# The low parts of the expert weights: one GpSimd subtraction of 1088 columns as two of 544

## The chip, the cores and the metric

The kernel runs on one core of a Trainium2 chip. The metric is the device time of one execution in microseconds (us), median of several runs. The engines are TensorE (PE), VectorE (DVE), ScalarE (ACT), GpSimd (POOL) and SyncE (SP), each with its own instruction stream; they meet only in semaphores.

## The reference

Input x has 2 x 1024 tokens of 256 features. The result is the sum of x, a log-space gated recurrence on the normalised x, and a mixture of 8 experts with the top 2 of each token:

```
xn = layernorm(x)
out = x + attn(xn) + ffn(xn)
# attn: k = xn @ W_z.T + b_z; cumsum over features, cumlogsumexp over time,
#       one mean and deviation over everything, exp, + xn, layernorm * ln_w + ln_b
# ffn, for each expert e of 8 (hidden 704):
h = silu(x @ w1[e].T) * (x @ w3[e].T)
out = out + h @ w2[e].T * expert_weight
```

## The kernel before

The first 63 us normalise x, compute the router's choice and the projections of the attention part. Then follow the expert tiles: the tokens are sorted by expert into tiles of 128, each tile belonging to one expert, 36 tiles (j = 0 to 35) in this input. All engines run the same loop over j, and the attention part is spread over the tiles by hand (functions `between`, `after`, `exp_log_first` and so on, with fixed tile numbers).

One tile goes like this. TensorE multiplies the gathered rows with w1 and w3 (`up`, 18 products at L1301), transposes the next tile's rows (L1270), multiplies the previous tile's hidden values with w2 (`down`, 18 products at L1319), and transposes the gated values (`h_tile`, 6 at L1331). ScalarE takes the silu (L608), copies the high part of x (L575), scales the result of `down` (L634), copies the high part of the transposed h (L603). VectorE multiplies the gate (L976), forms the low part of x (L967) and of h (L971), and in between does the attention's long elementwise steps on 128x1024 (L936, L941, L994, L1006, L1013), its scans (L983, L1000) and the last normalisation (L1069, L1074). TensorE's transposes (L1331) wait for the gate L976, that waits for L608.

Every product is made of fp32r values in two parts, high and low, so each weight is held as a high part and a low part. An expert's weights, WALL = 4352 columns, come by DMA into `raw` (SyncE, L339, and a small tail, L341) and are split in PIECES = 4 pieces of WP = 1088 columns: ScalarE rounds a piece to its high part (L617), GpSimd forms the low part as raw minus high (L425). Both do so behind a tile, in `split_due`: a table `plan` made on the chip says how many pieces are to be done before which tile (two at the start of an expert, one behind each of the next two tiles, for the next expert). Expert 0 is split by VectorE at the start; 7 experts x 4 pieces = 28 are done in the loop. GpSimd signals each piece (`s_w`); TensorE waits for it before it uses the expert, and SyncE before it loads the next expert's raw weights over that piece. ScalarE starts on an expert when all five loads of it have landed (`s_raw`).

GpSimd's stream in a tile is: gather of the rows of tile j + 4 (L390, an indirect DMA), scatter of tile j - 1 into the result with addition (L406), then the pieces due. Scatters wait for the landing of the one before. In tiles 28, 30 and 32 the attention part is added to the result by plain DMAs with addition (L414, `add_attention`), which also wait for scatters and are waited for by them, and there the pieces come before the scatter (`split_first`). The last tile's scatter is L470.

Of the kernel before, what the change touches and what calls it, by code (L numbers as in the profile page):

```python
# [32 lines left out]
WALL = WMAIN + D  # L33
LOADS = 5 * 16
PARTS_OF_H = 4
PIECES = 4
WP = WALL // PIECES
# [15 lines left out]
def build_program(nc, x, small, w_main, w_tail, out, xn_dram):  # L53
    fp32, f32r, i32 = mybir.dt.float32, mybir.dt.float32r, mybir.dt.int32
    u32, bf16 = mybir.dt.uint32, mybir.dt.bfloat16
    ALU, ACT, AX = mybir.AluOpType, mybir.ActivationFunctionType, mybir.AxisListType
    ds = bass.ds
    ctx = ExitStack()
    with ctx:
        def sb(name, shape, dt=fp32):  # L60
            return ctx.enter_context(nc.sbuf_tensor(name, shape, dt))

        def sem(name):
            return ctx.enter_context(nc.semaphore(name))
# [12 lines left out]
        wflat = wbuf[:, :, :, :].rearrange("p s h n -> p (s h n)")  # L77
        raw = sb("raw", [P, WALL])
# [61 lines left out]
        at = [0]  # L140
# [106 lines left out]
        s_w = sem("expert_pieces_ready")  # L247
# [42 lines left out]
        def hold(eng, s, value):  # L290

            eng.wait_ge(s, value)
            eng.nop(nofuse=True)
# [14 lines left out]
            if end:  # L308
                end(used)

        def wslot(e, part, a):

            return wflat[:, ds(e % 2 * (2 * WALL) + (a + part * WALL), WP)]


        @block.sync
# [28 lines left out]
        def _(pool):  # L345
            n = [0]
# [70 lines left out]
            def split_due(before, j):  # L417

                done = pool.value_load(plan[0:1, ds(j + 1, 1)], min_val=0, max_val=PIECES * (E - 1))
                with pool.If(before < done):  # L420
                    with pool.Fori(before, done) as p:
                        part = pool.snap(p % PIECES * WP)
                        hold(pool, s_hi, p + (PIECES + 1))
                        lo, hi = (wslot(p // PIECES + 1, n, part) for n in (1, 0))
                        pool.tensor_tensor(lo, raw[:, ds(part, WP)], hi.bitcast(fp32), ALU.subtract).then_inc(s_w, 1)  # L425
                return done

            for j in range(DEEP + 1):
# [1 line left out]
            pool.wait_ge(s_idx, 1)  # L430
            pool.wait_ge(s_ctl, 1)
            split_due(0, 0)

            def tile(i, u, done=None, parts=PARTS_OF_H, split_first=False):

                j = LOOP * i + (1 + u)
                if j + DEEP < NTILES:
                    gather(j + DEEP)
                if done is None:
                    done = pool.value_load(plan[0:1, ds(j, 1)], min_val=0, max_val=PIECES * (E - 1))  # L440
                if split_first:
                    done = split_due(done, j)
                scatter(j - 1, parts)
                return done if split_first else split_due(done, j)
# [32 lines left out]
        def _(act):  # L477
# [132 lines left out]
            def split_due(before, j):  # L610

                done = act.value_load(plan[0:1, ds(j + 1, 1)], min_val=0, max_val=PIECES * (E - 1))
                with act.If(before < done):
                    with act.Fori(before, done) as p:
                        part = act.snap(p % PIECES * WP)
                        hold(act, s_raw, p // PIECES * LOADS + 2 * LOADS)
                        act.activation(wslot(p // PIECES + 1, 0, part), raw[:, ds(part, WP)], ACT.Copy).then_inc(s_hi, 1)  # L617
                return done
# [817 lines left out]
```

## Time and profile before

| | |
|---|---|
| median of 3 runs | 352.63 us (350.98 to 352.78) |
| profiled execution | 352.66 us, span of the instructions 350.8 us |
| TensorE busy | 323.4 us (92%) |
| VectorE busy | 243.4 us (69%) |
| ScalarE busy | 229.2 us (65%) |
| GpSimd busy | 204.4 us (58%) |
| GpSimd's 28 subtractions (L425) | 78.7 us, mean 2822 ns |

Busy time of an engine includes time in which an instruction had begun and stood still, as for a port. Matmul ends are modelled. A time in a timeline is the start from the beginning of the span.

### The profile page before, as it was taken

What the parts mean: (1) busy time and instruction counts of PE and PEld (TensorE: products, weight loads), DVE (VectorE), ACT (ScalarE), POOL (GpSimd) and SP (SyncE); (2) the same over time, 40 slices, a digit from 0 to 9 for tenths busy, and PEclk for the clock granted to TensorE, in tenths of its full rate; (3) what the DMA queues carried; (4) which work ended last, traced back from release to release, by engine and by line L of the source; (5) the groups of instructions that cost most, each with busy time, mean ns of one, the idle gap of its engine ahead of it and who ended that gap; (6) DMA issues with size and microseconds to landing.
All of it is one profiled execution on the core that took longest, in us unless ns stands there. A gap on an engine that the chain in (4) does not pass through costs nothing.

```text
span 350.8 us, 6683 instructions
## 1 busy us (share of the span) xinstructions
PE 323.4 (92%) x1964; PEld 272.7 (78%) x1964; DVE 243.4 (69%) x430; ACT 229.2 (65%) x365; POOL 204.4 (58%) x137
## 2 busy tenths in 40 slices
PE   8998999898999999899989899999999999999950
PEld 8773474587878889788878788789998997999940
DVE  5488778989996779959889942455498767553410
ACT  2548898564889993899974349963955565443420
POOL 4600004249977763897789927765398458863531
PEclk9999969999999999999999999999999999999995
DMA  7952922005434642345346432544265265456431
GB/s 258 347 215 94 308 87 60 17 0 160 101 98 92 167 97 48 76 101 141 58 87 164 98 56 41 142 105 101 33 157 139 61 77 92 50 90 84 56 49 15
DMA packets 19087, 37.01 MB, mean 105 GB/s; under 512 B 2272, under 2 KB 13536, under 8 KB 19008
## 3 DMA queue, kind: packets, MB, share of 16 engines
q0 software_dynamic: 9168, 11.97, 21.7%
q1 hardware_dynamic: 8496, 22.56, 20.7%
q10 hardware_dynamic: 1376, 1.85, 1.5%
q8 instruction: 29, 0.48, 0.6%
q14 instruction: 18, 0.15, 0.1%
HBM read 27.45 MB, written 11.03 MB: 110 GB/s over the span
## 4 chain that ended last, share of the span: by engine, by line
PE 28%; issue 17%; ACT 15%; DVE 15%; DMA 13%; POOL 6%; POOLq 2%; ACTq 2%; DVEq 0%
PE PS L1301 9%; DMA out<-work,sidx 7%; PE PS L1195 7%; DMA out<-xrow 5%; PE PS L1319 4%; ACT L718 3%; POOL work L390 2%; PE PS L1331 2%; POOL out L406 2%; DVE tmp L976 2%; ACT tmp L608 2%; ACT L710 2%; ACT wbuf L617 2%; DVE hT L971 2%; DVE A L1013 1%
## 5 line engine op out<-in xcount | busy, mean ns | idle before, releaser
L1301 PE MATMUL PS<-wbuf,xT 128*128 128x512 f32 (+1 forms) x648 | 148.0, 382 | 4.4 <-issue 3.5
L1301 PEld LDWEIGHTS PS<-wbuf,xT 128*128 128x128 f32 x648 | 117.2, 188 | 28.3 <-issue 8.7
L425 POOL TENSOR_TENSOR wbuf<-raw,wbuf x28 | 78.7, 2822 | 27.4 <-ACT wbuf L617 26.6
L406 POOL DMA_INDIRECT out<-work,sidx x35 | 62.2, 1778 | 46.9 <-ACT work L634 24.8
L1319 PE MATMUL PS<-wbuf,hT 128*128 128x256 f32 x648 | 86.8, 288 | 0.0
L1319 PEld LDWEIGHTS PS<-wbuf,hT 128*128 128x128 f32 x648 | 79.3, 189 | 1.9 <-issue 1.9
L390 POOL DMA_INDIRECT work<-xn_dram,gidx x39 | 51.2, 1312 | 50.2 <-DVE gidx L907 36.8
L971 DVE TENSOR_TENSOR hT<-PS,hT 128x768 fp32r<-128x768 f32 x36 | 34.2, 950 | 46.1 <-ACT hT L603 45.1
L608 ACT ACTIVATE tmp<-PS 128x512 f32<-128x512 f32 x72 | 31.6, 459 | 38.8 <-PE PS L1301 38.7
L976 DVE TENSOR_TENSOR tmp<-tmp,PS 128x512 f32<-128x512 f32 x72 | 34.9, 515 | 28.8 <-ACT tmp L608 27.9
L1331 PE MATMUL PS<-ident,tmp 128*128 128x128 f32 x216 | 30.2, 276 | 6.1 <-DVE tmp L976 6.0
L634 ACT ACTIVATE work<-PS,wrow 128x256 f32<-128x256 f32 x35 | 16.4, 469 | 29.3 <-PE PS L1319 29.3
L603 ACT ACTIVATE hT<-PS 128x768 fp32r<-128x768 f32 x35 | 28.3, 810 | 10.5 <-PE PS L1331 10.5
L617 ACT ACTIVATE wbuf<-raw x28 | 30.4, 1110 | 4.7 <-issue 4.6
L1195 PE MATMUL PS<-xnT_M,small_sb 128*128 128x512 f32 x64 | 31.0, 624 | 1.7 <-ACT tmp L528 1.0
L1331 PEld LDWEIGHTS PS<-ident,tmp 128*128 128x128 f32 x216 | 23.9, 141 | 8.7 <-DVE tmp L976 7.7
L1195 PEld LDWEIGHTS PS<-xnT_M,small_sb 128*128 128x128 f32 x64 | 12.1, 202 | 14.0 <-issue 12.8
L710 ACT ACT_TABLE_LOAD x14 | 18.0, 1283 | 0.3
L718 ACT ACT_TABLE_LOAD x14 | 18.0, 1283 | 0.2
L967 DVE TENSOR_TENSOR xT<-PS,xT 128x256 fp32r<-128x256 f32 x37 | 15.5, 418 | 0.1
L575 ACT ACTIVATE xT<-PS 128x256 fp32r<-128x256 f32 x37 | 14.0, 382 | 1.6 <-PE PS L1270 1.6
L581 ACT ACTIVATE wrow<-work,first_pick 128x1 f32<-128x1 f32 x37 | 14.1, 385 | 0.0
(186 smaller groups left out, 367.3 us busy)
## 6 DMA issues: line engine op xcount, KB each, us to landing
raw<-w_main SPq DMA_DIRECT2D x24, 544.0 KB, 4.0
raw<-w_main SPq DMA_DIRECT2D x8, 416.0 KB, 3.5
xn_dram<-xrow SPq DMA_DIRECT2D x4, 516.0 KB, 5.9
out<-xrow POOLq DMA_DIRECT2D x4, 512.0 KB, 6.5
xrow<-x ACTq DMA_DIRECT2D x4, 256.0 KB, 5.8
xrow<-x SPq DMA_DIRECT2D x4, 256.0 KB, 5.2
small_sb<-small ACTq DMA_DIRECT2D x1, 768.0 KB, 8.3
work<-xn_dram,gidx POOLq DMA_INDIRECT x39, 4.1
```

What stands on the lines that cost most here:

```text
L390: pool.indirect_dma_start(xg[:, k, :], None, xn_dram, bass.IndirectOffsetOnAxis(gidx[:, j:j + 1], 0)).then_inc(s_gt[k], 16)
L406: pool.indirect_dma_start(out, bass.IndirectOffsetOnAxis(sidx[:, j:j + 1], 0), ysb[:, j % DEEP, :], None, compute_op=ALU.add).then_inc(s_s ...
L425: pool.tensor_tensor(lo, raw[:, ds(part, WP)], hi.bitcast(fp32), ALU.subtract).then_inc(s_w, 1)
L608: act.activation(sls[n], w1_ps[n], ACT.Silu).then_inc(s_silu, 1)
L617: act.activation(wslot(p // PIECES + 1, 0, part), raw[:, ds(part, WP)], ACT.Copy).then_inc(s_hi, 1)
L718: act.preload_act_table_set("silu_and_others")
L971: dve.tensor_tensor(hT[:, 1, :], hT_ps, hT[:, 0, :].bitcast(fp32), ALU.subtract).then_inc(s_hlo, 1)
L976: dve.tensor_tensor(g_hs[n], sls[n], w3_ps[n], ALU.mult).then_inc(s_g, 1)
L1195: ins = pe.matmul(PS[:, base + qo * CH:base + (qo + 1) * CH], wzh_sb[:, q, mat, qo * P:(qo + 1) * P], xnT[:, q, c * CH:(c + 1) * CH], star ...
L1301: ins = pe.matmul(PS[:, at:at + cols], xT[:, slot, xpart, q * P:(q + 1) * P], wbuf[:, w, wpart, q * 2 * F + at:q * 2 * F + at + cols], sta ...
L1319: ins = pe.matmul(y_ps, hT[:, hpart, c * P:(c + 1) * P], wbuf[:, w, wpart, W13 + c * D:W13 + (c + 1) * D], start=(c == 0 and hpart == 0 an ...
L1331: ins = pe.transpose(hT_ps[:, c * P:(c + 1) * P], g_h[:, a:a + P], ident[:, :])
```

## The change

Each piece is subtracted by two instructions of 544 columns, first half and second half, in place of one of 1088. The wait for ScalarE stands ahead of the first, the signal `s_w` behind the second. `wslot` gets a length.

```
-        def wslot(e, part, a):
+        def wslot(e, part, a, n=WP):
 
-            return wflat[:, ds(e % 2 * (2 * WALL) + (a + part * WALL), WP)]
+            return wflat[:, ds(e % 2 * (2 * WALL) + (a + part * WALL), n)]
...
                         part = pool.snap(p % PIECES * WP)
                         hold(pool, s_hi, p + (PIECES + 1))
-                        lo, hi = (wslot(p // PIECES + 1, n, part) for n in (1, 0))
-                        pool.tensor_tensor(lo, raw[:, ds(part, WP)], hi.bitcast(fp32), ALU.subtract).then_inc(s_w, 1)
+                        for at in (0, WP // 2):
+                            lo, hi = (wslot(p // PIECES + 1, n, part + at, WP // 2) for n in (1, 0))
+                            ins = pool.tensor_tensor(lo, raw[:, ds(part + at, WP // 2)], hi.bitcast(fp32), ALU.subtract)
+                        ins.then_inc(s_w, 1)
```

The instructions on GpSimd in the body of that loop, before (`hi_pieces_ready` is the semaphore `s_hi` that ScalarE signals; ISA rows are register instructions on the queue):

```order
L421 ISA
L425 ISA [waits hi_pieces_ready]
L425 ISA x2
L425 TENSOR_TENSOR wbuf<-raw,wbuf 128x1088
L421 REGISTER_ALU
L421 COMPARE_AND_BRANCH
```

and of the changed kernel, at the same place:

```order
L421 ISA
L426 ISA [waits hi_pieces_ready]
L426 ISA x2
L426 TENSOR_TENSOR wbuf<-raw,wbuf 128x544
L426 ISA x2
L426 TENSOR_TENSOR wbuf<-raw,wbuf 128x544
L421 REGISTER_ALU
L421 COMPARE_AND_BRANCH
```

Two register instructions and one subtraction have come in; nothing waits between the two. No instruction of another engine has moved; lines below L425 are two higher.

## Rows read from the trace of the kernel before

**Rows 1.** The page, busy time of TensorE: us, share, instructions.

```profile
PE 323.4 (92%) x1964; PEld 272.7 (78%) x1964; DVE 243.4 (69%) x430; ACT 229.2 (65%) x365; POOL 204.4 (58%) x137
```

**Rows 2.** Timeline of TensorE: start us, us, instruction, [idle before <-releaser].

```profile
84.54 0.88 PE L1331 MATMUL PS<-ident,tmp 128*128 128x128 f32 x6 [0.58 <-DVE tmp L976]
...
147.52 0.88 PE L1331 MATMUL PS<-ident,tmp 128*128 128x128 f32 x6 [1.15 <-DVE tmp L976]
148.79 4.12 PE L1301 MATMUL PS<-wbuf,xT 128*128 128x512 f32 x18 [0.40 <-issue]
...
193.88 0.88 PE L1331 MATMUL PS<-ident,tmp 128*128 128x128 f32 x6 [0.94 <-DVE tmp L976]
...
270.21 0.88 PE L1331 MATMUL PS<-ident,tmp 128*128 128x128 f32 x6
271.22 4.11 PE L1301 MATMUL PS<-wbuf,xT 128*128 128x512 f32 x18
...
313.50 0.82 PE L1331 MATMUL PS<-ident,tmp 128*128 128x128 f32 x6
314.07 4.10 PE L1301 MATMUL PS<-wbuf,xT 128*128 128x512 f32 x18
```

**Rows 3.** Timeline of VectorE, instructions with two operands in SBUF.

```profile
85.00 4.05 DVE L941 TENSOR_TENSOR U<-U,tmp 128x1024 f32<-128x1024 f32 x1
...
136.67 1.22 DVE L994 TENSOR_TENSOR U<-U,xnT_M 128x1024 f32<-128x1024 f32 x1
...
143.31 3.56 DVE L994 TENSOR_TENSOR U<-U,xnT_M 128x1024 f32<-128x1024 f32 x1
...
185.94 3.98 DVE L1006 TENSOR_TENSOR U<-U,xnT_M 128x1024 f32<-128x1024 f32 x1
...
266.18 3.38 DVE L1074 SCALAR_TENSOR_TENSOR xrow<-xrow,rstd,small_sb 128x256 f32<-128x256 f32 x2
...
281.43 0.88 DVE L1074 SCALAR_TENSOR_TENSOR xrow<-xrow,rstd,small_sb 128x256 f32<-128x256 f32 x2
```

**Rows 4.** Timeline of GpSimd, two pieces of tile 10.

```profile
143.16 2.63 POOL L425 TENSOR_TENSOR wbuf<-raw,wbuf  x1 [0.42 <-issue]
...
145.74 3.48 POOL L425 TENSOR_TENSOR wbuf<-raw,wbuf  x1
```

**Rows 5.** Line L425: ns min/median/max, first and last start.

```profile
L425 POOL TENSOR_TENSOR wbuf<-raw,wbuf x28: 2504/2600/3522, 74.7 to 306.0; - x28
```

**Rows 6.** The chain that ended last (two rows), then GpSimd's timeline.

```profile
284.63 9.10 DMA out<-xrow
...
293.76 0.28 POOL wbuf L425
...
288.82 5.22 POOL L425 TENSOR_TENSOR wbuf<-raw,wbuf  x2 [0.92 <-ACT wbuf L617]
...
303.30 1.37 POOL L414 DMA_DIRECT2D out<-xrow  x1 [0.49 <-issue]
...
342.63 1.57 POOL L470 DMA_INDIRECT out<-hst,scol  x1 [3.02 <-DMA out<-work,sidx]
```

**Rows 7.** GpSimd's groups by form: busy us, mean ns of one.

```profile
L464 POOL COPY scol<-sidx 128x1 uint32 x1 | 0.4, 379 | 0.0
...
L1427 POOL MEMSET const-float32-1.0<- 128x1 f32 x1 | 0.1, 101 | 0.0
```

**Rows 8.** ScalarE's timeline; then a window: us, ScalarE busy, clock, DMA.

```profile
148.43 0.81 ACT L603 ACTIVATE hT<-PS 128x768 fp32r<-128x768 f32 x1 [0.77 <-PE PS L1331]
...
148.40:178.40 30.00, 29.76 (x42) 1.00 0.42 99
```

**Rows 9.** SyncE's tail load, its time to landing (DMA issues), ScalarE's next rounding.

```profile
95.79 0.49 SPq L341 DMA_DIRECT2D raw<-w_tail  x1
...
raw<-w_tail SPq DMA_DIRECT2D x8, 64.0 KB, 3.8
...
105.09 2.11 ACT L617 ACTIVATE wbuf<-raw  x2
```

## The prediction

> **What bounds the kernel now.** I read the busy shares first, then the waits of each engine, then the timelines of TensorE, VectorE, GpSimd and ScalarE side by side for each of the 28 pieces (L425), and last the chain of work that ended last. TensorE is busy 92% of the span [rows 1], and in the expert tiles an undisturbed tile runs without a gap: its transposes (L1331) at 313.50 are followed by the next tile's first product (L1301) 0.57 us later [rows 2]. Time is lost where the transposes wait for VectorE's gate (L976): 0.58 us before 84.54, 1.15 before 147.52, 0.94 before 193.88. Such a wait costs twice, since the next L1301 then comes not 0.57 but 1.27 us (147.52 to 148.79) or 1.01 us (270.21 to 271.22) after the transposes [rows 2].
>
> Why is the gate late? An undisturbed 128x1024 subtraction on VectorE (L994) takes 1.22 us. The same line takes 3.56 us at 143.31; a like one takes 4.05 us at 85.00 and 3.98 us at 185.94, and a pair of L1074 takes 3.38 us at 266.18 against 0.88 us at 281.43 [rows 3]. All read two operands from SBUF, and each overlaps a piece on GpSimd. At 143.31 the piece had begun at 143.16 and ended at 145.79 [rows 4]; VectorE's ended at 146.87, 1.08 us behind it, about its own length. So VectorE stood still for the whole of the piece. The other direction shows too: the next piece is recorded from 145.74, 3.48 us long instead of 2.50 to 2.60 [rows 4, 5]: it was held until VectorE's ended, and then needed 149.22 - 146.87 = 2.35 us. Whoever has begun runs to its end.
>
> The end of the kernel is set by another chain. The scatters (L406) and the additions of the attention part (L414) all go through GpSimd one behind the other, each waiting for the landing of the last. From about 284 us on, the chain that ended last is theirs, and the last scatter (L470) waited 3.02 us for a DMA [rows 6]. TensorE's last stretch has room beside it.
>
> **The change, step by step.**
> 1. *GpSimd's own time.* 28 instructions of 1088 columns (2.50 us undisturbed, [rows 5]) become 56 of 544. The columns are the same; what is added is one start-up, f, per piece. The trace has no 544-column form. From below, a one-column memset takes 0.10 us in all; from above, a one-column copy takes 0.38 us [rows 7], which also holds a wait for the scatter beside it. I take f = 0.2, between the two and nearer the memset. That makes a half 1.35 us and adds 28 x 0.2 = 5.6 us to GpSimd. The Trainium skill (GPSIMD Engine Reference, section 3.1) gives 4497 ns for a two-input operation of 2048 columns; with the 2504 ns of 1088 columns here an estimate of f is 0.25 us, which would put the sum 0.1 to 0.2 us higher. The two register instructions ahead of the second half run on the queue under the first half (1.35 us), so I cost them at nothing; uncovered they would be some 0.3 us a piece.
> 2. *The pieces with nothing of VectorE's on them* (13 of 28, as I count them on the two timelines: those from 107 to 125, at 153, from 214 to 261 and the last at 306) cost nothing: TensorE is not waiting for the weights there, and the raw weights are reloaded early.
> 3. *The stall of VectorE.* If VectorE gets in between the halves, it waits at most 1.35 us for the first half and the second half waits for it. Piece by piece:
>  - **At 143.** The first half ends at 144.5, L994 ends at 145.7 instead of 146.87, the gate comes 1.15 us earlier. TensorE's wait of 1.15 goes and about 0.3 of the lengthened 1.27 [rows 2]. But ScalarE is the next late: its L603 began at 148.43 after a wait of 0.77 [rows 8], so it was free 0.77 earlier, and from 148.4 to 178.4 it was busy 29.76 of 30.00 us, up to the next place where TensorE waits. So only about 0.85 us comes through (0.77 and the slack of an issue). What the pieces at 153 and 161 free in the same stretch counts nothing, for the same reason.
>  - **At 75 to 97.** The wait of 0.58 before 84.54 and 0.6 of the longer gap behind it go: 1.2 us. The stall of 2.8 us at 85.00 [rows 3] shrinks too, and could give 0.7 more. Against it: here GpSimd's pieces are pushed behind VectorE's, the fourth by 3 to 4 us by my reckoning (four halves, each behind an operation of 1.2 us or a scan). Its last load (tail, L341) was issued at 95.79 and lands 3.8 us later at 99.6; ScalarE needs it at 105.09 [rows 9]. Of 5.5 us of room 1.5 is eaten by ScalarE being earlier and up to 4 by the piece. I take 1.3 of 1.9.
>  - **At 178 to 200.** VectorE's sequence is L1006, L971, L1013, statistics, gate, nearly without a gap. At 185.94 it stood 2.76 us; with the piece before it shifted by one half, L1006 runs before the next one starts and L1013 pays up to 1.35. The gate at 193 comes over 1.2 us earlier: wait of 0.94 and about 0.45 of the longer gap, 1.4 us [rows 2, 3]. The gates of the tile before and the tile behind are late for the same cause; I count 0.3 us for each, a choice below half of this site. Together 2.0.
>  - **At 266.** The second L1074 stood 2.50 us and stands half as long. L1331 at 270.21 had no wait on record but the longer gap: 1.01 - 0.57 = 0.44, and 0.2 of being late itself: 0.65.
>  Sum before 284 us: 0.85 + 1.3 + 2.0 + 0.65 = 4.8 us.
> 4. *The end chain.* At 288.82 two pieces (5.22 us) stand on GpSimd ahead of a scatter. The addition before that scatter landed at 293.73 and the second piece ended at 294.04: the piece was last, by 0.3 [rows 6]. It gets two start-ups, 0.4, and an L1074 of 0.44 us comes between its halves where 0.3 of waiting was: +0.15. The next piece ended at 302.81, 0.49 us ahead of L414 at 303.30, which stood behind it [rows 6]: +0.2. The third has room. So +0.75 us, with f = 0.10 +0.45, with f = 0.38 +1.3. That TensorE also gains at 292 is worth nothing, since this chain ends last.
>
> Sum: the profiled execution took 352.66 us (span 350.8); 352.66 - 4.8 + 0.75 = 348.6 us. Its time is that of the median of the three runs, 352.63, so I forecast 348.6, 1.1% faster. The case's own range is 346.9 to 350.6: 4.8 may be 2.8 (the sites at 85 and 193 at 0.3 and 1.0) or 6.2 (at 1.9 and 2.8), with 0.75 and 0.45 for the end chain.
>
> **The rivals.**
> - *ScalarE takes it back.* ScalarE is gapless over long stretches, and the load of the site at 75 to 97 comes late. Then the sites at 143 and 85 give nothing: 352.66 - 2.65 + 0.75 = 350.8 us. For it: the wait of 0.77 only on ScalarE [rows 8]; against it: ScalarE itself starts from TensorE's transposes, so an earlier tile moves it too. 0.17.
> - *The port is not given up between the halves; slower.* Two instructions of one piece have no semaphore and no loop step between them. If GpSimd starts the second before the first is drained at all, VectorE stands for both. Then no site gains, and the end chain pays three start-ups; at f between 0.2 and 0.38 plus a stretched L1074 that is 0.6 to 1.4 us: 353.3 to 354.1 us. It decides if VectorE's long rows still stand 2.5 us. Against it: the second piece at 145.74 was dispatched 0.05 us before the first ended at 145.79, and VectorE still went ahead of it [rows 4]. 0.15.
>  The Trainium skill (GPSIMD Engine Reference, section 2.1) says that a core starts on the next instruction as soon as it has done its own share, while others still work on the last. That would argue for this rival; the row at 145.74 is the trace's answer, though for two instructions with loop steps between them.
> - *The change does nothing to VectorE but moves its stalls.* Where several two-operand operations follow one another, each may meet a half: twice 1.35 for once 2.5. This is inside the range of the first two cases, not apart from them.
>
> **Chances.** Forecast 0.68, ScalarE 0.17, port kept 0.15. A measurement of this kernel tells 0.5% (1.8 us) from no change: the bounds are 350.9 and 354.4. The ScalarE case lies on the upper side of faster, so half of it counts there: faster 0.68 + 0.07 = 0.75; slower needs the kept port at its upper price and a late load of weights with it, 0.06; same 0.19. The range 346.6 to 352.8 takes in the forecast's own range and the ScalarE case, and leaves out most of the kept port and the far tail of the gain.
>
> **What the profile after would show.** Step 1: 56 rows of 544 columns, 1.30 to 1.45 us undisturbed, and GpSimd's sum for the line near 78.7 + 5.6 and what it waits more for VectorE. Step 3: no two-operand instruction of VectorE of 1024 columns longer than 1.2 + 1.4 us; the waits of L1331 for L976 mostly gone; ScalarE's chain from 148 on 0.85 us earlier than the tile count alone explains. Step 4: the scatter behind the two pieces later by 0.5 us or so relative to the additions before it. Wrong would be: stalls of 2.5 us still there; a new wait of ScalarE (L617) for the raw weights at about 103; or a start-up much above 0.38.

## The result, and the profile after

The changed kernel takes 354.46 us (median of 9 runs, 353.35 to 356.85), the kernel before on the same chip 351.89 us (9 runs, 350.98 to 352.89): a ratio of 1.0075, 95% interval 1.0048 to 1.0101. It is slower by 2.6 us; 348.6 us was forecast, and the range ended at 352.8. A second measurement of the same kernel, among the experiments, gave 354.46 us and 1.0052 (1.0031 to 1.0073). The profiled execution took 355.73 us, with a span of 353.9 us against 350.8; it lies 1.3 us above its median, the profiled execution before 0.8 above its own, so the profiles differ by 3.1 us and the medians by 2.6.

The page after, to be held against [rows 1]: TensorE has 2.8 us more busy time for the same 1964 products, VectorE 0.5 us less, GpSimd 6.3 us more.

```profile
PE 326.2 (92%) x1964; PEld 275.1 (78%) x1964; DVE 242.9 (69%) x430; ACT 229.8 (65%) x365; POOL 210.7 (60%) x165
...
L426 POOL TENSOR_TENSOR wbuf<-raw,wbuf x56 | 85.8, 1649 | 24.2 <-ACT wbuf L619 22.9
```

**Start at VectorE**, with its timeline, since that is what the edit aims at. The first four rows answer to [rows 3]; then follow three more sites and, at 158.44, an undisturbed scan for comparison. Lines are two higher than before.

```profile
85.74 4.17 DVE L943 TENSOR_TENSOR U<-U,tmp 128x1024 f32<-128x1024 f32 x1
...
144.33 1.22 DVE L996 TENSOR_TENSOR U<-U,xnT_M 128x1024 f32<-128x1024 f32 x1
...
187.52 4.12 DVE L1008 TENSOR_TENSOR U<-U,xnT_M 128x1024 f32<-128x1024 f32 x1
...
268.05 4.00 DVE L1076 SCALAR_TENSOR_TENSOR xrow<-xrow,rstd,small_sb 128x256 f32<-128x256 f32 x2
...
93.04 5.23 DVE L985 TENSOR_TENSOR_SCAN xnT_M<-U,u 128x1024 f32<-128x1024 f32 x1
...
158.44 2.28 DVE L1002 TENSOR_TENSOR_SCAN U<-tmp,U 128x1024 f32<-128x1024 f32 x1
...
162.62 5.66 DVE L1002 TENSOR_TENSOR_SCAN U<-tmp,U 128x1024 f32<-128x1024 f32 x1
...
179.78 1.70 DVE L1008 TENSOR_TENSOR U<-U,xnT_M 128x1024 f32<-128x1024 f32 x1
```

The subtraction at 85.74 stands 4.17 - 1.22 = 2.95 us (before 2.83), that at 187.52 stands 2.90, the pair at 268.05 stands 3.12 (before 2.50), and the scan at 162.62 stands 5.66 - 2.28 = 3.38 us, where before it stood 1.32. These are not stalls of one half (1.35 us). But the row at 179.78 stands only 0.48, and that at 144.33 not at all. So halving works at some places and not at others. Taken over all of VectorE's instructions (length minus the undisturbed length of the same line), the stalls sum to about 22.4 us before and 21.9 us after; such a sum depends by some 2 us on what is taken for undisturbed, the difference between two kernels much less, and VectorE's busy time on the page falls by the same 0.5 us. Halving has moved the stalls and hardly made them less.

**Then GpSimd at the same places.** The next fence is its timeline, in narrow windows, so that a group of two halves can be seen one by one.

```profile
84.41 1.72 POOL L406 DMA_INDIRECT out<-work,sidx  x1 [0.30 <-issue]
85.58 1.94 POOL L426 TENSOR_TENSOR wbuf<-raw,wbuf  x1
86.89 1.94 POOL L426 TENSOR_TENSOR wbuf<-raw,wbuf  x1
...
161.82 1.59 POOL L406 DMA_INDIRECT out<-work,sidx  x1 [0.31 <-issue]
162.88 3.24 POOL L426 TENSOR_TENSOR wbuf<-raw,wbuf  x2
...
177.70 1.37 POOL L426 TENSOR_TENSOR wbuf<-raw,wbuf  x1 [0.43 <-issue]
179.01 1.38 POOL L426 TENSOR_TENSOR wbuf<-raw,wbuf  x1
...
144.26 8.49 POOL L426 TENSOR_TENSOR wbuf<-raw,wbuf  x4 [0.50 <-issue]
```

Behind a scatter, a half is recorded 0.55 us before the scatter's record ends (85.58 against 84.41 + 1.72 = 86.13). Its record is 1.94 us long instead of 1.37, and the second half is recorded from 86.89, 0.63 us before the first ends at 87.52. The two lie over each other, and VectorE stands for both. With the four halves at 177.70, which come behind an idle gap, the second is recorded from 179.01, 0.06 us before the first ends at 179.07, and VectorE gets in: 0.48 us of stall at 179.78. The start-up f can be read here too: two halves in step are 179.01 + 1.38 - 177.70 = 2.69 us against 2.50 to 2.54 of a whole piece, f = 0.15 to 0.19. Undisturbed pairs over the whole trace give about 0.14.

**Last TensorE**, timeline, to be held against [rows 2].

```profile
85.29 0.86 PE L1333 MATMUL PS<-ident,tmp 128*128 128x128 f32 x6
...
147.31 0.82 PE L1333 MATMUL PS<-ident,tmp 128*128 128x128 f32 x6
...
169.28 0.95 PE L1321 MATMUL PS<-wbuf,hT 128*128 128x256 f32 x6 [0.35 <-DVE hT L973]
171.96 0.87 PE L1333 MATMUL PS<-ident,tmp 128*128 128x128 f32 x6 [1.73 <-DVE tmp L978]
...
195.61 0.87 PE L1333 MATMUL PS<-ident,tmp 128*128 128x128 f32 x6 [0.93 <-DVE tmp L978]
...
272.70 0.87 PE L1333 MATMUL PS<-ident,tmp 128*128 128x128 f32 x6 [0.68 <-DVE tmp L978]
...
70.58 5.67 PE L1303 MATMUL PS<-wbuf,xT 128*128 128x512 f32 x18 [1.21 <-issue]
```

The waits before 85.29 and 147.31 are gone. That before 195.61 has stayed (0.94 before), and two are new: 1.73 us before 171.96, behind the scan that stood 3.38 us, and 0.68 us before 272.70. The last row shows 18 products that take 5.67 instead of 4.11 us. The windows (columns: us, then TensorE, its loads, VectorE, ScalarE and GpSimd busy, the granted clock, and the DMA engines' share and GB/s) say why, and that it happens twice:

```profile
70.50:76.30 5.80, 5.72 (x21) 4.76 (x21) 4.75 (x8) 3.43 (x5) 1.16 (x1) 0.71 0.01 3
...
172.90:178.70 5.80, 5.72 (x21) 4.76 (x22) 4.24 (x6) 5.64 (x7) 4.48 (x3) 0.71 0.49 63
...
148.90:153.00 4.10, 4.10 (x26) 3.69 (x25) 1.01 (x2) 4.07 (x5) 3.95 (x4) 1.00 0.36 105
```

The mean clock of both stretches is 0.71; inside them it stands at 0.50, the lower of its two levels (1.2 GHz), for some 3 us (71.0 to 74.0 is all at 0.50), and the 18 products take 1.55 us more each time. The profiled execution before has no such stretch in its tiles. The second one begins behind the start of tile 14's products at 172.98: tile 13, for all its 9.80 us, ran at the full clock. Tile 14 took 8.41 us against 8.37 before, so there the slow products stand where a wait of 0.89 us for the gate and the gap behind it had been; what tile 14 would have taken at the full clock, no run shows. TensorE's timeline of the kernel before there:

```profile
178.04 0.87 PE L1331 MATMUL PS<-ident,tmp 128*128 128x128 f32 x6 [0.89 <-DVE tmp L976]
```

**The bill.** I take the start of each tile's 18 products (L1301, L1303) in both timelines; the first column is what the stretch added (after minus before), the second what the prediction had.

| stretch | us | predicted |
|---|---|---|
| up to tile 1 | +0.56 | 0 |
| tiles 1 to 4 ("At 75 to 97"), with the low clock in tile 1 (+1.55) | +0.44 | -1.3 |
| tiles 5 to 9 | +0.10 | 0 |
| tiles 10 to 12 ("At 143"): -2.01, +0.50, +0.65 | -0.86 | -0.85 |
| tile 13, all at the full clock | +2.06 | 0 |
| tiles 14 to 17 ("At 178 to 200"), with the low clock in tile 14 (up to +1.55) | -0.45 | -2.0 |
| tiles 18 to 25 | +0.02 | 0 |
| tile 26 ("At 266") | +0.63 | -0.65 |
| end chain, from the scatter at 281.93 to L472 | +0.48 | +0.75 |
| behind L472 | +0.12 | 0 |
| sum | +3.10 | -4.05 |

The chain of scatters at the end, on GpSimd's timeline (to be held against [rows 6]; the scatter at 281.93 stood at 279.43 before):

```profile
281.93 1.59 POOL L406 DMA_INDIRECT out<-work,sidx  x1 [5.71 <-ACT work L636]
...
291.33 5.56 POOL L426 TENSOR_TENSOR wbuf<-raw,wbuf  x4 [0.92 <-ACT wbuf L619]
...
345.61 1.58 POOL L472 DMA_INDIRECT out<-hst,scol  x1 [2.99 <-DMA out<-work,sidx]
```

Two terms came out as predicted, the end chain and the site at 143. The rest did not. The theory from here on, **theory A**: where the halves start out of step behind a scatter, the second has begun before the first has ended, and VectorE stands for the whole piece as before. Its rivals: **B**, it isn't the hold but the additional GpSimd time (start-ups) that costs; **C**, the loss is one of timing alone, pieces pushed onto other operations of VectorE, and **D**, it is the low clock, by chance, and not the edit.

### The profile page after: what moved, and what is told of

Same layout as the page of the kernel before. It is cut to its first block, busy times and chain, and to the rows that moved or that the text cites. A ratio compares the mean times of both kernels' runs of the same rounds, so it can differ in the third digit from the quotient of the medians.

```text
span 353.9 us, 6767 instructions
## 1 busy us (share of the span) xinstructions
PE 326.2 (92%) x1964; PEld 275.1 (78%) x1964; DVE 242.9 (69%) x430; ACT 229.8 (65%) x365; POOL 210.7 (60%) x165
## 3 DMA queue, kind: packets, MB, share of 16 engines
q10 hardware_dynamic: 1376, 1.85, 1.5%
## 4 chain that ended last, share of the span: by engine, by line
PE 41%; DVE 16%; issue 13%; DMA 13%; ACT 7%; POOL 5%; POOLq 2%; ACTq 0%; SPq 0%; DVEq 0%
PE PS L1303 16%; PE PS L1321 8%; PE PS L1197 7%; DMA out<-work,sidx 6%; DMA out<-xrow 4%; PE PS L1333 4%; POOL wbuf L426 3%; DVE tmp L978 2%; DVE xnT_M L985 1%; DVE U L1002 1%; DVE hT L973 1%; POOL work L390 1%; DVE xrow L1076 1%; DVE A L1015 1%; PE PS L1227 1%
## 5 line engine op out<-in xcount | busy, mean ns | idle before, releaser
L1303 PE MATMUL PS<-wbuf,xT 128*128 128x512 f32 (+1 forms) x648 | 151.1, 387 | 3.5 <-issue 2.7
L1303 PEld LDWEIGHTS PS<-wbuf,xT 128*128 128x128 f32 x648 | 119.5, 192 | 27.7 <-issue 7.3
L426 POOL TENSOR_TENSOR wbuf<-raw,wbuf x56 | 85.8, 1649 | 24.2 <-ACT wbuf L619 22.9
L1197 PE MATMUL PS<-xnT_M,small_sb 128*128 128x512 f32 x64 | 31.9, 640 | 1.4 <-ACT tmp L530 1.0
L1197 PEld LDWEIGHTS PS<-xnT_M,small_sb 128*128 128x128 f32 x64 | 12.4, 206 | 14.3 <-issue 13.1
```

The source lines that it names most:

```text
L426: ins = pool.tensor_tensor(lo, raw[:, ds(part + at, WP // 2)], hi.bitcast(fp32), ALU.subtract)
L1197: ins = pe.matmul(PS[:, base + qo * CH:base + (qo + 1) * CH], wzh_sb[:, q, mat, qo * P:(qo + 1) * P], xnT[:, q, c * CH:(c + 1) * CH], star ...
L1303: ins = pe.matmul(PS[:, at:at + cols], xT[:, slot, xpart, q * P:(q + 1) * P], wbuf[:, w, wpart, q * 2 * F + at:q * 2 * F + at + cols], sta ...
```

## The experiments

### A wait between the halves

GpSimd waits until its own first half has ended before it issues the second.

```
                             ins = pool.tensor_tensor(lo, raw[:, ds(part + at, WP // 2)], hi.bitcast(fp32), ALU.subtract)
+                            if at == 0:
+                                ins.then_inc(s_half, 1)
+                                hold(pool, s_half, p + 1)
                         ins.then_inc(s_w, 1)
```

> The changed kernel, with a semaphore between the halves: GpSimd signals the first half and waits for it before it starts the second. In the profile of the changed kernel VectorE stood 2.9 to 3.4 us where the piece stood right behind a scatter (at 85.7, 93.0, 162.6, 187.5, 268.5), and the records of the two halves overlap there by 0.6 us; elsewhere they overlap by 0.04 us and VectorE gets in. Theory A (GpSimd's cores are out of step behind a scatter, so the port is never free between the halves): with the wait no two-operand instruction of VectorE stands longer than 2.0 us, VectorE's total of stalls falls from 23 us to about 15, and the time falls by 2 to 4 us, to 350.5 to 352.5. Theory B (the port is kept between instructions for another reason, as that GpSimd, when it has work queued, always goes first): stalls near 2.5 us stay and the wait only adds some 0.1 to 0.2 us a piece, time 354 to 356.

Measured: 350.62 us (348.85 to 352.20, 12 runs) against 352.08 before, ratio 0.9961 (0.9937 to 0.9985). GpSimd's timeline, then VectorE's and ScalarE's:

```profile
86.16 1.95 POOL L427 TENSOR_TENSOR wbuf<-raw,wbuf  x1
88.57 1.36 POOL L427 TENSOR_TENSOR wbuf<-raw,wbuf  x1 [0.45 <-POOL wbuf L427]
...
85.43 1.22 DVE L947 TENSOR_TENSOR U<-U,tmp 128x1024 f32<-128x1024 f32 x1
...
88.67 3.39 DVE L989 TENSOR_TENSOR_SCAN xnT_M<-U,u 128x1024 f32<-128x1024 f32 x1
...
103.59 2.11 ACT L623 ACTIVATE wbuf<-raw  x2 [1.36 <-DMA raw<-w_tail]
```

The halves of a piece are now 0.45 us apart everywhere, no instruction of VectorE stands longer than 1.2 us, and the stalls sum to 12.6 us instead of 21.9. GpSimd has more to do than in the changed kernel (the wait comes 28 times), and the kernel is 3.8 us faster than that one's 354.46: B falls, A stands. The rounding of ScalarE at 103.59 now waits 1.36 us for the raw weights' tail, the new wait that the prediction named; tile 5 takes 9.09 us instead of 7.71 for it. The same kernel, measured a second time:

> The kernel with the wait between the halves of every piece once more, for comparison on the same chip: 350.6 us, 349.8 to 351.4, 0.3 to 0.5% below before, halves 0.45 us apart, no stall of VectorE above 1.4 us, and again the wait of ScalarE (L623) for the raw weights' tail near 103 us of about 1.4. If the ratio comes out above 0.9985, the gain of this version is not to be told from no change.

Measured: 350.31 us (349.22 to 351.29, 10 runs) against 352.65, ratio 0.9942 (0.9919 to 0.9965). No stall above 1.2 us, and the sum 12.4. The wait for the tail wasn't there in this execution, whose tiles began 1.1 us later and held a stretch of low clock at 70 us, so that part of the expectation was wrong; what decides it, no run shows.

### The same out-of-step start taken away by other means

A one-column memset with a signal, waited for, stands ahead of each piece; the halves themselves are those of the change.

```
                         hold(pool, s_hi, p + (PIECES + 1))
+                        pool.memset(scol[:, 0:1], 0).then_inc(s_half, 1)
+                        hold(pool, s_half, p + 1)
```

> The changed kernel, with a one-column memset of GpSimd ahead of each piece that is signalled and waited for, so that all cores are in step before the first half; nothing between the halves. Theory A: the records of the halves overlap by 0.04 us everywhere, VectorE gets in between them at every place, no stall above 2.0 us; GpSimd starts a piece up to 0.6 us later, but it then ends at the same time as now. Time 350.5 to 353. Theory B: stalls of 2.9 us stay, time 354.5 to 356.

Measured: 356.80 us (354.83 to 358.73, 6 runs), ratio 1.0121 (1.0085 to 1.0156). GpSimd's timeline behind a scatter, and TensorE's a little later:

```profile
87.10 0.70 POOL L425 MEMSET scol<- 128x1 uint32 x1
88.46 4.64 POOL L429 TENSOR_TENSOR wbuf<-raw,wbuf  x2 [0.67 <-POOL scol L425]
...
93.48 5.66 PE L1306 MATMUL PS<-wbuf,xT 128*128 128x512 f32 x18 [1.97 <-POOL wbuf L429]
```

The mechanism of A is there: the halves follow one another with 0.04 us of overlap at every piece, no instruction of VectorE stands over 1.2 us, and the stalls sum to 11.5 us. Yet it is the slowest kernel of all, and the expected 350.5 to 353 us was wrong. Behind a scatter the step ahead takes 0.70 + 0.67 us, so the pieces come late, TensorE waits 1.97 us for the weights themselves (the third piece of that expert, 88.46 + 4.64 = 93.10), and the 18 products after it take 5.66 us again, in a stretch of low clock (0.50 from 94 to 97). Stalls removed are worth nothing where the piece is then awaited by TensorE. At this site the prediction had weighed late pieces against ScalarE's next load alone, not against TensorE.

### Quarters

```
-                        for at in (0, WP // 2):
-                            lo, hi = (wslot(p // PIECES + 1, n, part + at, WP // 2) for n in (1, 0))
-                            ins = pool.tensor_tensor(lo, raw[:, ds(part + at, WP // 2)], hi.bitcast(fp32), ALU.subtract)
+                        for at in range(0, WP, WP // 4):
+                            lo, hi = (wslot(p // PIECES + 1, n, part + at, WP // 4) for n in (1, 0))
+                            ins = pool.tensor_tensor(lo, raw[:, ds(part + at, WP // 4)], hi.bitcast(fp32), ALU.subtract)
```

> Four instructions of 272 columns a piece, one signal behind the last. It prices the start-up f of an instruction and tells the two theories apart. The uncontended halves show f = 2 x 1.34 - 2.52 = 0.14 to 0.16 us. Theory A: a piece alone takes 2.52 + 3 x 0.15 = 2.97 us; behind a scatter the cores stay out of step over all four, the port is kept, and VectorE stands 3.2 to 3.8 us there; elsewhere it stands at most 0.75 us. The end chain gets 3 pieces x 0.45 = 1.3 us against the kernel before. Time 353 to 357. Theory B: VectorE stands about 3 us at every place. A third, that the smaller parts let VectorE in everywhere: no stall above 0.8 us, and a time under that of the kernel before, 348 to 350.

Measured: 354.10 us (352.55 to 355.42, 12 runs), ratio 1.0055 (1.0034 to 1.0076). GpSimd's and VectorE's timeline:

```profile
87.12 3.53 POOL L426 TENSOR_TENSOR wbuf<-raw,wbuf  x4
...
87.61 4.12 DVE L943 TENSOR_TENSOR U<-U,tmp 128x1024 f32<-128x1024 f32 x1
```

Behind a scatter the four quarters still keep VectorE out for 2.90 us. A quarter by itself, 272 columns, takes 0.77 us. The longest stall of this kernel is 3.97 us, of a subtraction at 177.97 over the eight quarters of two pieces. Cutting finer doesn't help where the parts aren't in step.

### What the piece is worth at most

The whole piece is formed by one instruction of 32 of its 1088 columns; the low part of the other 1056 is left out. A memset at the start of the kernel, not shown in the cut, puts zeros there. The lines with a minus are those of the kernel before.

```
-                        lo, hi = (wslot(p // PIECES + 1, n, part) for n in (1, 0))
-                        pool.tensor_tensor(lo, raw[:, ds(part, WP)], hi.bitcast(fp32), ALU.subtract).then_inc(s_w, 1)
+                        lo, hi = (wslot(p // PIECES + 1, n, part, 32) for n in (1, 0))
+                        pool.tensor_tensor(lo, raw[:, ds(part, 32)], hi.bitcast(fp32), ALU.subtract).then_inc(s_w, 1)
```

> The kernel before, with only 32 of the 1088 columns of each piece subtracted (28 instructions; the other low parts stay at the zeros that GpSimd writes once at the start, in a time in which it waits). It leaves out nearly all of GpSimd's work on the weights, so it bounds what any cut of the pieces can win. If VectorE's stalls cost TensorE what the prediction counted (4.8 us before the end chain, and 0.5 in it), 346 to 348 us; if ScalarE takes most of it back, 349.5 to 351.

Measured: 348.06 us (347.22 to 349.94, 6 runs) against 352.08, ratio 0.9899 (0.9863 to 0.9935), at the upper edge of the 346 to 348 expected if TensorE gets the whole. Page, and GpSimd's timeline:

```profile
PE 321.7 (93%) x1964; PEld 273.7 (79%) x1964; DVE 221.5 (64%) x430; ACT 229.0 (66%) x365; POOL 130.4 (38%) x138
...
272.91 1.59 POOL L407 DMA_INDIRECT out<-work,sidx  x1 [4.42 <-ACT work L635]
...
337.94 1.57 POOL L471 DMA_INDIRECT out<-hst,scol  x1 [2.91 <-DMA out<-work,sidx]
```

VectorE is busy 21.9 us less than before: that is what the pieces cost it, and near the 22.4 us worked out from its instructions one by one. TensorE reaches tile 27 at 264.71, 6.5 us earlier, and the scatter at 272.91 is 6.5 us earlier as well; the last one, at 337.94, only 4.7. The end chain, which is made of landings, gives 1.8 of it back. With no piece at all in the way some 4.0 us are to be had by the median. The forecast of -4.0 thus asked halving for all that there is. By site this bound is -2.50 us for tiles 1 to 4, -0.83 for tiles 10 to 12, -0.50 for tile 13, -2.52 for tiles 14 to 17 and -0.66 for tile 26.

### Which pieces lose it

First the changed kernel again, then halving in the first two of each expert's four pieces alone, and in the last two alone (the others whole), by a branch on `p % PIECES < 2`.

```
+                        with pool.If(p % PIECES < 2):
+                            subtract(2, False)
+                        with pool.Else():
+                            subtract(1, False)
```

Here `subtract(k, wait)` forms the piece in k instructions; in the second kernel the 2 and the 1 are exchanged.

> The changed kernel once more, with a profile of its own, to see what repeats. In its first profile two tiles of TensorE (at 70.6 and at 173.0) ran in a stretch with a granted clock of 0.71 and took 5.66 instead of 4.1 us for their 18 products; that is 3.1 us, as much as the whole difference of the two profiled executions. If these stretches belong to the change, the one at 173, behind a wait of 1.73 us for the gate, is there again; if they are chance, neither need be, and the kernel without them takes about 352.6. The stalls of 2.9 us behind the scatters, the one of 3.4 us of the scan at about 162, and the free halves in tile 10 should be there again. Time 353.5 to 355.

> Only the first two pieces of an expert in halves (they mostly follow the roundings of ScalarE, not a scatter), the other two whole as before; a branch on the piece's number is added to GpSimd's queue in all. Theory A (cores out of step behind a scatter keep the port): the halves are used where they help, VectorE's stalls fall by 3 to 5 us, TensorE gains at tiles 2 and 29, the end chain pays 0.3: time 350 to 351.7, not above the kernel before. If the cost is the start-up or the queue alone, it is paid for half of the pieces: 353 to 353.5.

> The other half: the last two pieces of each expert in halves (they mostly stand right behind a scatter), the first two whole. Theory A: the port is kept over both halves, each start-up of 0.14 us is added to the stalls, so stalls of 2.9 to 3.4 us, nothing gained: 352.3 to 354. If position does not matter, the same as the kernel with the first two halved.

Measured: the changed kernel 354.46 us (353.26 to 354.97, 12 runs) against 352.45, ratio 1.0052 (1.0031 to 1.0073); first two halved 353.14 (351.04 to 355.39, 12), 1.0023 (0.9998 to 1.0049); last two halved 352.02 (350.41 to 354.16, 12), 0.9986 (0.9960 to 1.0012). The latter two can't be told from before. Both lie outside what was expected of them (350 to 351.7 and 352.3 to 354): what theory A by itself promised for the first two did not come.

Then all pieces halved, with the wait between the halves in the last two alone, and in the first two alone:

```
+                                if not at:
+                                    ins.then_inc(s_half, 1)
+                                if wait and not at:
+                                    hold(pool, s_half, p + 1)
...
+                        with pool.If(p % PIECES < 2):
+                            subtract(2, False)
+                        with pool.Else():
+                            subtract(2, True)
```

In the second of the two, False and True are exchanged.

> All pieces in halves, and the wait for the first half between the halves of the last two pieces only. With the wait in all pieces the time was 350.6 and ScalarE waited 1.4 us for raw weights at 103.6, since GpSimd's pieces came later (0.46 us for each wait). Here four of the eight waits of that stretch are gone: ScalarE's wait falls to under 0.8 us, stalls stay near 12 us in sum, and the time is 349.5 to 351. A branch on the piece's number is added to GpSimd's queue.

> All pieces are halved; GpSimd waits for the first half to have ended only in the first two pieces of an expert (the branch is that of the run with the wait in the last two, turned round). Theory (VectorE stands for both halves where the halves start out of step behind a scatter, and each such stall longer than one half that lies in front of a gate costs TensorE): the stalls of 2.8 us and more are gone at the first two pieces and stay at the third (one to three of them, near 178 to 200 and 95); tile 13 takes 7.2 to 7.8 us instead of 9.80 and TensorE keeps its clock there, since what made that tile long were the first two pieces. The wait in both pairs was worth 3.8 us and that in the last two 1.5, so if the two add, 352.1 us here, 351.3 to 352.8. Rival (only the first two matter, the last two pieces' stalls are absorbed): as the kernel with both waits, 350.6, up to 351.2. Rival (the branch itself and not the place of the wait was what cost the kernel with the wait in the last two): 353 again.

Measured: wait in the last two 352.98 (350.84 to 354.46, 12), 1.0019 (0.9993 to 1.0045), not to be told from before, where 349.5 to 351 had been expected; wait in the first two 354.74 (352.67 to 356.77, 12) against 352.65, ratio 1.0074 (1.0050 to 1.0099): as slow as the changed kernel. My expectation of the last one (352.1) was wrong, and with it the reading that tile 13 is the fault of the first two pieces alone. (It also lost 1.3 us at tile 17, 9.61 instead of 8.30, under stalls of 2.07 and 2.91 us at 187.19 and 192.89.) The tiles, from starts of the 18 products in each profile, show why:

| kernel | tile 10 | tile 13 | tile 15 | scan ahead of the piece at tile 13 |
|---|---|---|---|---|
| before | 8.85 | 7.74 | 7.45 | -1.07 |
| changed, both profiles | 6.84 | 9.80 | 6.84 and 6.86 | 0.26 and 0.24 |
| first two halved | 6.87 | 9.67 | 6.85 | 0.24 |
| last two halved | 8.86 | 7.25 | 7.54 | -0.85 |
| halved, wait in the first two | 6.87 | 10.22 | 6.87 | 0.68 |
| halved, wait in the last two | 6.84 | 7.24 | 9.97 | 0.74 |
| halved, both waits | 7.68 and 6.84 | 7.23 and 7.17 | 6.86 | 1.06 and 1.06 |
| quarters | 6.85 | 7.57 | 9.61 | 1.00 |
| halved, step ahead | 6.87 | 7.25 | 7.70 | -1.11 |

The last column is the start of the piece on GpSimd minus the start of the scan (L1000 of the kernel before) on VectorE, us.

Tile 10 holds the first two pieces of an expert, tile 13 the fourth. Halving the first two takes the stall at 143 away (6.84 to 6.87), and in four profiles tile 13 then takes 9.7 to 10.2 us. The last column tells which: where the scan's record begins 0.24 to 0.68 us ahead of the piece's, the scan stands for all of the piece; where it begins 0.74 to 1.06 us ahead, it runs clean (2.28 to 2.32 us). So in the kernels with a wait in the last two, and with quarters, tile 13 is short because GpSimd came later still and the scan ran ahead of the piece. One of them is at 0.74, only 0.06 us from the profile at 0.68 that lost. The wait itself was not put to the test there. The timelines of GpSimd and VectorE there, before:

```profile
158.07 1.59 POOL L406 DMA_INDIRECT out<-work,sidx  x1 [0.31 <-issue]
161.32 2.52 POOL L425 TENSOR_TENSOR wbuf<-raw,wbuf  x1 [1.66 <-ACT wbuf L617]
...
162.39 3.60 DVE L1000 TENSOR_TENSOR_SCAN U<-tmp,U 128x1024 f32<-128x1024 f32 x1
```

and with the first two halved and the fourth whole:

```profile
157.20 3.03 POOL L390 DMA_INDIRECT work<-xn_dram,gidx  x1 [0.17 <-issue]
160.53 1.59 POOL L406 DMA_INDIRECT out<-work,sidx  x1 [0.30 <-issue]
161.58 3.12 POOL L427 TENSOR_TENSOR wbuf<-raw,wbuf  x1
...
161.34 5.53 DVE L1010 TENSOR_TENSOR_SCAN U<-tmp,U 128x1024 f32<-128x1024 f32 x1
...
170.54 0.88 PE L1341 MATMUL PS<-ident,tmp 128*128 128x128 f32 x6 [1.74 <-DVE tmp L986]
```

Before, the piece came 1.66 us behind the scatter, having waited for ScalarE; it began 1.07 us ahead of the scan, which stood for the rest of it, 1.32 us. With the first two halved, GpSimd lags: its four halves at tile 10 took 8.49 us in the changed kernel (2.63 + 3.48 less 0.05 of overlap before, 6.06) because VectorE's subtraction and a scan went in between. Being late, the gather of that tile falls on VectorE's scan of 157.15 to 159.43 and takes 3.03 us; before, it stood at 156.78, ahead of the scan, and took 0.99. So scatter and piece run at once behind one another, the piece is recorded 0.24 us behind the scan's start, and the scan stands for all of it: 5.53 - 2.28 = 3.25 us. TensorE then waits 1.7 us for the gate, and in all four profiles with this wait its next 18 products ran at a clock of 0.71; in the profiles without it (before, last two halved, wait in the last two, both waits twice) they ran at 1.00. That is C, and it is one part of the answer. With the last two halved alone, the piece comes before the scan, at 161.92, behind a wait of 1.74 us for ScalarE as in the kernel before, and in step, and the scan stands 0.36 us. What the wait between the halves is worth is read at tile 15 instead. Where it was given to the last two alone, the hold came back there, in the first pieces of the next expert:

```profile
174.88 5.63 POOL L428 TENSOR_TENSOR wbuf<-raw,wbuf  x4
...
176.07 5.54 DVE L1018 TENSOR_TENSOR U<-U,xnT_M 128x1024 f32<-128x1024 f32 x1
...
185.57 0.87 PE L1343 MATMUL PS<-ident,tmp 128*128 128x128 f32 x6 [2.00 <-DVE tmp L988]
```

The same place with both waits:

```profile
174.98 1.78 POOL L427 TENSOR_TENSOR wbuf<-raw,wbuf  x1
...
176.18 1.68 DVE L1012 TENSOR_TENSOR U<-U,xnT_M 128x1024 f32<-128x1024 f32 x1
```

In both, VectorE's subtraction comes 1.2 us behind the start of a first half that is out of step. Without a wait the four halves lie over each other by 0.41 us, across the loop step between the two pieces too, and it stands 4.32 us; with the wait it gets in behind the first half and stands 0.46. Two more such pairs: 0.20 us into a first half it stands 2.90 us without a wait (changed, 187.52) and 1.58 with it (wait in the last two, 192.27); 1.49 us into it, 1.60 (changed, 196.07) and 0.30 (wait in the last two, 186.03). At these places the pairs differ in the wait alone, and they show A.

Less stalling is not less time, though: with the wait in the last two VectorE is busy 233.2 us, 1.2 us less than with both waits, and the kernel is 2.4 us slower than that one. The 4.32 us of stall gave TensorE 2.00 us of wait, here at an undisturbed clock. So a wait of that length alone doesn't bring the clock down. What does, no run shows.

D falls in the main. The mean granted clock is on record for every execution, and at the same mean clock (0.971) six executions of the changed kernel average 354.44 us and five of the kernel before in the same series 352.86: 1.6 of the 2.0 us between the two medians are there at an equal clock. The stretch at 172 us was in every profile with the long tile 13, so it hangs on the edit. That at 70 us was in both profiles of the changed kernel, that with quarters and one of the two with both waits, and in none of the other eight. It begins at 70.58, ahead of the first piece (75.14), so no piece can have brought it. How often a kernel meets it, and whether the change bears on that at all, stays open; up to 1.55 us of the 3.1 between the two profiles may be no effect of the edit.

## Why the prediction was wrong

- **Bounds of the kernel: right, but for one.** A stalled gate costs twice, and the end chain ends last; both show again. "Whoever has begun runs to its end" does not hold of the recorded starts: the scan at 162.62 began 0.26 us ahead of the piece and stood for it.
- **Step 3, "If VectorE gets in between the halves, it waits at most 1.35 us": this step failed.** The sum took it for granted at every site that VectorE gets in. It does where the piece begins behind an idle gap or another piece in step (stalls of 0.48 at 179.78, none at 144.33). Behind a scatter both halves hold, and all five stalls of over 2.8 us are of this kind. The prediction had this as its second rival, and weighed against it the row at 145.74 [rows 4], where VectorE went ahead. That row is a piece behind a piece, in step. The rows that would have told are those of pieces straight behind a scatter, on GpSimd's timeline of the kernel before: 3.13 us long, not 2.50, and begun before the scatter's record ends.

```profile
83.68 1.72 POOL L406 DMA_INDIRECT out<-work,sidx  x1 [0.30 <-issue]
84.83 3.13 POOL L425 TENSOR_TENSOR wbuf<-raw,wbuf  x1
```

  That rival's 353.3 to 354.1 us is near the measured 354.46 by luck: it had only the end chain pay, by 0.6 to 1.4, which came to +0.48; the rest is tile 13, which it didn't have either.

  The rule of the Trainium skill that the rival named (GPSIMD Engine Reference, section 2.1, a core starts on the next instruction as soon as it has done its own share) agrees with the overlap of 0.63 us at 86.89 and with 0.06 where the halves are in step. That the cores are out of step by the scatter is only argued; that a wait between the halves or a step ahead of them restores the gap is shown.
- **"At 143", -0.85: right in size, not in kind.** The tile gained 2.01 us, since VectorE's subtraction ran ahead of the first half (144.33 beside a half recorded from 144.26) instead of behind it. 1.15 came back in the next two tiles, so that -0.86 was left. With 32 columns a piece, where nothing of VectorE stands, the same three tiles give -0.83: there was no more to be had. That ScalarE or another engine is the next late was right.
- **"At 178 to 200", -2.0: -0.45.** The rows at 187.52 and 196.07 stood 2.90 and 1.60 us, where at most 1.35 was counted. In the -0.45 are also the slow products of tile 14, with up to 1.55 us; how much of the miss is theirs, no run shows.
- **"At 75 to 97", -1.3: -1.1 without the low clock.** All of it came in tiles 1 and 2 (-1.39 without the low clock); tiles 3 and 4, under the stalls of 2.95 us at 85.74 and 2.89 at 93.04, lost 0.28.
- **"At 266", -0.65: +0.63.** The pair stood 3.12 instead of 2.50, for both halves behind a scatter.
- **A site that stood in the sum at nothing: tile 13, +2.06.** The prediction named its piece ("the pieces at 153 and 161") only for what it could free, and called moved stalls "inside the range of the first two cases". That was wrong. The stall went from 1.32 to 3.38 us when GpSimd's piece slid by 1.3 us against the scan, from 1.07 ahead of it to 0.26 behind, and in tile 14 the clock fell behind it. In all four profiles with the long tile 13 the gain at tile 10 is there too; but the gain doesn't bring it by necessity, since four other profiles have the one without the other (quarters, step ahead, wait in the last two, one with both waits).
- **Step 1, f = 0.2: near, 0.14 to 0.19.** GpSimd's line went from 78.7 to 85.8 us on the page, as said (84.3 and what it waits more).
- **Step 2: right for the change**, no wait for weights on TensorE; the experiment with a step ahead of each piece shows how near it is.
- **Step 4, +0.75: +0.48**, mostly by the smaller f.

The size of the whole: 350.8 + 3.1. Of the 3.1 us, 2.06 are tile 13, and the sites where a gain was expected gave 0.24 us together instead of 4.8 (1.79 without the low clock of the first, and up to 1.55 more without that in tile 14).

## What to carry to other kernels

Cutting an instruction that keeps another engine out helps only if something keeps the cuts apart: between two instructions of GpSimd without a wait the second may already have begun. Look at what stands ahead of the instruction, and compare its length there with its length after a gap. Here a wait on its own first half, 0.45 us, turned +0.5 to +0.75% into -0.4 to -0.6%.

A stall's price depends on where a piece lands, so any edit that changes an engine's pace moves the pieces behind it. Work out a moved stall at the next sites as a term of its own, with its worst case, and not as spread: here up to 3.8 us for one piece of 3.12, and 4.3 for two pieces out of step.

## What the runs showed of the hardware that I had not expected

- A subtraction of GpSimd recorded straight behind its scatter begins 0.55 us before the scatter's record ends and lasts about 0.6 us longer (1.94 instead of 1.37 for 544 columns, 3.13 instead of 2.50 for 1088); the next one behind it keeps that overlap (0.63 us), in quarters over all four. Where VectorE holds the first of them up, the rest are in step: the first quarter at 162.86, straight behind a scatter, took 1.85 us, and the next lay over it by 0.04.
- The order of the records doesn't say who has the port. At 144.33 VectorE went ahead of a half recorded 0.07 us earlier; at 162.62 it stood for a piece recorded 0.26 us later, with the wait in the first two for one recorded 0.68 us later. Begun 0.76 us ahead of its piece, a subtraction stood 3.76 us in one kernel (first two halved, 86.19) and not at all in another (wait in the last two, 85.31).
- A wait on the engine's own signal costs GpSimd 0.45 us between two subtractions; a one-column memset with such a wait, straight behind a scatter, takes 0.70 + 0.67 us.
- The granted clock fell to its lower level for about 3 us, 1.55 us more for 18 products, behind a wait of 1.73 us on TensorE in four profiles of four and behind one of 1.97 us with the step ahead, but not behind one of 2.00 us in another kernel.
